# Attention with transposed scores: keys on the partitions, row maxima found in a pass of their own

## What is computed

```
xq = rms_norm(x @ wq.T, q_norm_w)         # 32 heads of 64
xk = rms_norm(x @ wk.T, k_norm_w)         # 8 key heads, each used by 4 query heads
xv = x @ wv.T
scores = einsum('bhtd,bhsd->bhts', xq, xk) / 8 + slope_h * (s - t)   # -inf unless 0 <= t - s <= 256
attn = softmax(scores)
out = einsum('bhts,bhsd->bhtd', attn, xv) @ wo.T
x = x + layernorm(out)
x = x + layernorm(ffn(layernorm(x)))      # silu(g) * u, inner width 1408
```

## Time and profile before

| what | value |
|---|---|
| median of 3 runs | 1387.37 us (1386.64 to 1392.79) |
| span of the profiled execution | 1386.5 us |
| PE busy | 1249.0 us (90%), 7996 products |
| DVE busy | 960.8 us (69%) |
| ACT busy | 797.8 us (58%) |
| POOL busy | 362.5 us (26%) |
| DMA | 180.36 MB, 130 GB/s over the span |

### The profile page before, as it was taken

The page is one execution under the profiler, slowest core; times in us unless marked ns, Lnnn a source line. Parts: engine busy times, 40 slices in busy tenths (PEclk is TensorE's granted clock), DMA queues, the critical chain, the costliest instruction groups (busy, mean ns, idle before and its releaser), DMA issues.

```text
span 1386.5 us, 28786 instructions
## 1 busy us (share of the span) xinstructions
PE 1249.0 (90%) x7996; PEld 1049.7 (76%) x7996; DVE 960.8 (69%) x2514; ACT 797.8 (58%) x2141; POOL 362.5 (26%) x443
## 2 busy tenths in 40 slices
PE   5999999985888899999999999999799998989894
PEld 4778787864677778888888888888677786868683
DVE  4587777668888887888888888888553665262623
ACT  3555454545788888888888888888322322222221
POOL 1000000010366664344344344344211001020201
PEclk9999999995799999999999999999899999999997
DMA  4226262556344453454443354343433322020100
GB/s 152 99 103 230 104 246 106 216 194 244 138 157 159 159 188 114 141 171 155 134 156 127 130 170 156 133 155 122 141 106 121 107 92 91 1 71 21 40 22 32
DMA packets 94444, 180.36 MB, mean 130 GB/s; under 512 B 7456, under 2 KB 36256, under 8 KB 94368
## 3 DMA queue, kind: packets, MB, share of 16 engines
q1 hardware_dynamic: 94368, 179.42, 37.2%
HBM read 107.83 MB, written 71.57 MB: 129 GB/s over the span
## 4 chain that ended last, share of the span: by engine, by line
PE 54%; issue 23%; DVE 10%; DMA 4%; ACT 4%; POOL 2%; SPq 1%; DVEq 1%; ACTq 0%; POOLq 0%
PE bank L1141 16%; PE bank L1206 13%; PE bank L1163 8%; PE bank L1172 7%; PE bank L1268 4%; PE bank L1184 3%; DMA v_st<-v_scr 3%; PE bank L1195 2%; DVE u_sb L951 2%; PE bank L1186 2%; DVE inv_rms L905 1%; DVE pT_lo L958 1%; ACT p_sb L747 1%; DMA o_in<-o_scr 1%; DVE o_raw L972 1%
## 5 line engine op out<-in xcount | busy, mean ns | idle before, releaser
L747 ACT ACTIVATE p_sb<-u_sb,low 128x384 f32<-128x384 f32 (+2 forms) x512 | 274.9, 537 | 70.5 <-DVE low L951 46.6
L951 DVE CUSTOM_DVE_ANT_0 u_sb<-bank,bias 128x384 f32<-128x384 f32 (+2 forms) x512 | 232.1, 453 | 69.0 <-PE bank L1163 49.5
L1163 PE MATMUL bank<-k_st,q_st 128*128 128x384 f32 (+2 forms) x1024 | 254.8, 331 | 17.0 <-DMA v_st<-v_scr 11.3
L1172 PE MATMUL bank<-ident,p_sb 128*128 128x128 f32 x1152 | 225.8, 288 | 45.1 <-DVE pT_lo L958 40.1
L958 DVE TENSOR_TENSOR pT_lo<-bank,pT_hi 128x384 f16<-128x384 f32 (+2 forms) x512 | 231.3, 452 | 21.4 <-ACT pT_hi L755 11.6
L755 ACT ACTIVATE pT_hi<-bank 128x384 f16<-128x384 f32 (+2 forms) x512 | 206.3, 403 | 47.4 <-PE bank L1172 42.9
L1163 PEld LDWEIGHTS bank<-k_st,q_st 128*128 128x128 f32 x1024 | 180.8, 197 | 42.7 <-issue 9.2
L1172 PEld LDWEIGHTS bank<-ident,p_sb 128*128 128x128 f32 x1152 | 141.9, 144 | 86.5 <-ACT p_sb L747 41.3
L1184 PE MATMUL bank<-v_st,pT_hi 128*128 128x128 f16 x1152 | 171.9, 224 | 0.7 <-DVE pT_lo L958 0.7
L1268 PE MATMUL bank<-zT_hi,gu 128*128 128x512 f32 x440 | 161.6, 400 | 3.0 <-issue 1.7
L554 POOL TENSOR_TENSOR o_mid<-o_raw,inv_sum 128x256 f32<-128x256 f32 x128 | 79.4, 620 | 314.7 <-DVE o_raw L972 314.7
(11 more groups left out here) (108 smaller groups left out, 2303.7 us busy)
## 6 DMA issues: line engine op xcount, KB each, us to landing
q_scr<-qk SPq DMA_DIRECT2D x64, 512.0 KB, 2.7
q_st<-q_scr SPq DMA_DIRECT2D x32, 1024.0 KB, 5.8
k_st<-k_scr SPq DMA_DIRECT2D x64, 256.0 KB, 3.0
o_scr<-o_out SPq DMA_DIRECT2D x128, 128.0 KB, 1.7
o_in<-o_scr SPq DMA_DIRECT2D x16, 1024.0 KB, 8.4
k_scr<-qk SPq DMA_DIRECT2D x16, 512.0 KB, 2.7
x_in<-x SPq DMA_DIRECT2D x4, 1024.0 KB, 8.1
w_stage<-wqT SPq DMA_DIRECT2D x4, 1024.0 KB, 6.5
```

The costliest lines, as they stand in the source:

```text
L747: nc.scalar.activation(p_sb[:, u % RING, 0:w], u_sb[:, u % RING, 0:w], ACT.Exp, scale=-1.0, bias=low[:, u % RING:u % RING + 1], accum_out= ...
L951: nc.vector.tensor_tensor_reduce(out=u_sb[:, u % RING, 0:w], in0=bank[u % 2][:, 0:w], in1=bias[:, 2 * u // UNITS, u % REP, at:at + w], sca ...
L1163: mm = nc.tensor.matmul(bank[u % 2][:, 0:w], q_st[:, s, r, P * i:P * i + P], k_st[:, s, part, P * key:P * key + w], start=(part == 0), sto ...
L1172: mm = nc.tensor.transpose(bank[2 + u % 2][:, P * j:P * j + P], p_sb[:, u % RING, P * j:P * j + P], ident[:])
```

## The change

The attention stage is built anew, and what feeds it with it.

- **Scores stand transposed**: keys on the partitions, 4 heads x 128 queries = 512 columns. A unit is one block of 128 keys x 128 queries for the four heads of a key head: 9 blocks per key head (`BLOCKS`), 18 units per n instead of 32. `scores` makes them with two products of 512 columns; the second one's 100 rows hold the low part of the keys and, as rows of the contraction, slopes, distances, the maxima and the window's mask (`k2`, `q2`).
- **Row maxima come from a pass of their own** (`max_entry`, `find_max`), one key head ahead: 16 products of 32 to 288 columns per key head, DVE's add-and-extreme on each, then two small transposes (`turn`), a copy on ACT and a round trip through DRAM to turn them into row 67 of `q2`. ACT issues these transfers (`copy_low`, `load_low`).
- **No transposes of the probabilities**. `exps` reads PSUM, POOL zeroes what lies outside the window (`mask`, six of nine blocks), ACT rounds to f16 (`round_p`), DVE (4 of 9 blocks) or POOL (5 of 9) takes the rest (`split_p`). `weigh_values` makes 12 products of 64 or 65 columns per block; the 65th column is a column of ones in the values and gives the row's sum, so that `finish_o` on DVE inverts and multiplies once.
- **The norm of the values** goes into `wo` (`split_wo`, now on ACT and DVE) instead of into every output.
- **Stores and loads**: `q_scr` holds rows of 2048 columns per key head. `store_qk` stores four query chunks at a time in four transfers; ACT's copy into `raw` waits until the same chunks of the previous batch are stored (`lo_stored`). Per key head 12 transfers load what were 4 (`load_km`, `load_k1`, `load_q1`, `load_q2`, `load_v`); the query rows of `q2` are loaded as 64 and 3. Constant rows are built in f32 by POOL and copied by DMA.
- At the end of attention, `load_o` for the first tile of the tail is issued after all output stores have landed.

```diff
-UNITS = 2 * TT * REP
+BLOCKS = [(i, j) for i in range(TT) for j in range(max(0, i - NB + 1), i + 1)]
+GUNITS = len(BLOCKS)
+UNITS = 2 * GUNITS
+DVE_SPLITS = (0, 1, 4, 7)
+LAGS = {"scores": 0, "exps": 0, "mask": 0, "round": 1, "split": 2, "weigh": 3, "finish": 4}
+MAX_STEPS = [[("max", 0), ("max", 1)], [("max", 2), ("max", 3)], ...
+RING = 6
...
@@ SP @@
+                elif f % REP == REP - 1:
+                    for half in range(2):
...
+                        sp.dma_start(q_scr[group, 0:HD].rearrange("a d n -> (a d) n"),
+                                     raw[rows, REP * j:REP * j + REP].rearrange("p c n -> p (c n)")).then_inc(lo_stored[j], DMA)
+                        sp.dma_start(q_scr[group, HD:2 * HD].rearrange("a d n -> (a d) n"), qk[rows, j % 2].bitcast(F32)).then_inc(hi_stored[j % 2], DMA)
...
+            def load_q2(n, s):
+                for a, b in ((0, HD), (HD, HD + 3)):
+                    sp.dma_start(q2[a:b, s].bitcast(F32),
+                                 q_scr[bass.ds(2 * n + s, 1), HD + a:HD + b].rearrange("g r t -> (g r) t")).then_inc(q2_loaded[s], DMA)
...
+            attend(B * TT - 1, (2, TT - 2), last=True)
+            store_o(B * TT - 1, 1, [2, 3])
             for i in range(TT):
                 sp.wait_ge(o_stored[i], DMA * 2 * B * TT)
+            load_o(B - 2, TT - 1)
@@ POOL @@
+            def mask(n, u):
...
+                pool.wait_ge(p_ready, UNITS * n + u + 1)
                 hold(pool)
+                nc.gpsimd.affine_select(out=p, in_=p, compare_op=ALU.is_ge, fill=0.0, base=0,
+                                        pattern=[[0, REP], [sign, P]], channel_multiplier=-sign).then_inc(masked, 1)
+
+            def split_p(n, u):
+                if u % GUNITS in DVE_SPLITS:
+                    return
+                pool.wait_ge(p_hi_ready, UNITS * n + u + 1)
+                nc.gpsimd.tensor_tensor(out=p_lo[:, u % RING], in0=p_sb[:, u % RING], in1=p_hi[:, u % RING], op=ALU.subtract).then_inc(p_split[0], 1)
@@ ACT @@
-                        at_least(act, qk_ready, (QC + KVC) * (b - 1) + n + 1)
-                        nc.scalar.activation(raw[:, n], bank[n % 4][:], ACT.Copy).then_inc(raw_ready, 1)
+                        at_least(act, lo_stored[n // REP], DMA * (2 if n < QC else 4) * b)
...
+                        nc.scalar.activation(raw_at(n), short(bank[n % 4][:]), ACT.Copy).then_inc(raw_ready, 1)
...
+            def copy_low(n, s, h, bank_at):
...
+                nc.scalar.activation(lowT[0:NQ // 2, h], bank[bank_at][0:NQ // 2, 0:P], ACT.Copy).then_inc(lowT_ready, 1)
+                act.wait_ge(lowT_ready, 2 * g + h + 1)
+                act.dma_start(q_scr[bass.ds(g, 1), ROWS - 1, 2 * T * h:2 * T * h + 2 * T].rearrange("g (q c) -> (g q) c", c=P),
+                              lowT[0:NQ // 2, h]).then_inc(low_stored[h], DMA)
+
+            def load_low(n, s, h):
+
+                act.wait_ge(low_stored[h], DMA * (2 * n + s + 1))
+                act.dma_start(q2[HD + 3:HD + 4, s, 2 * T * h:2 * T * h + 2 * T].bitcast(F32),
+                              q_scr[bass.ds(2 * n + s, 1), ROWS - 1, 2 * T * h:2 * T * h + 2 * T]).then_inc(low_loaded[s][h], DMA)
@@ DVE @@
+            def find_max(n, s, q, bank_at):
+
+                w = min(SHORT * (q + 1), MAXW)
...
+                dve.wait_ge(m_psum, NQ * (2 * n + s) + q + 1)
+                hold(dve)
+                nc.vector.tensor_tensor_reduce(out=u_sb[:, q % 2, 0:w], in0=bank[bank_at][:, 0:w], in1=bias[:, s, MAXW - w:MAXW], scale=1.0, scalar=BIG,
+                                               op0=ALU.add, op1=ALU.min, accum_out=low[:, s, q:q + 1]).then_inc(u_ready, 1)
@@ PE @@
+                at_least(pe, p_ready, UNITS * n + u - 1)
+                nc.tensor.matmul(bank[u % 2][:], k1[:, s, keys], q1[:, s, queries], start=True, stop=False)
+                nc.tensor.matmul(bank[u % 2][:], k2[0:FIXED, s, k2_at:k2_at + P], q2[0:FIXED, s, queries],
+                                 start=False, stop=True).then_inc(s_psum, 1)
...
+                for r in range(REP):
+                    hi, lo = (x[:, u % RING, P * r:P * r + P] for x in (p_hi, p_lo))
+                    nc.tensor.matmul(acc[:, r], hi, v_st[:, s, j, HD:2 * HD + 1], start=(first and r == 0), stop=False, skip_group_check=True)
+                    nc.tensor.matmul(acc[:, r, 0:HD], hi, v_st[:, s, j, 0:HD], start=False, stop=False, skip_group_check=True)
+                    mm = nc.tensor.matmul(acc[:, r], lo, v_st[:, s, j, HD:2 * HD + 1], start=False, stop=(i == j), skip_group_check=True)
                 mm.then_inc(pv_done, 1)
```

More of the change, by code:

```diff
@@ L116, in due, with tiles_due, splits_before, max_bank @@
         nn, uu = (n, u - lag) if u >= lag else (n - 1, UNITS + u - lag)
-        if uu < UNITS and not (isinstance(nn, int) and nn < 0) and (stage not in OF_FOUR_HEADS or uu % REP == REP - 1):
+        if uu < UNITS and not (isinstance(nn, int) and nn < 0) and (stage != "finish" or uu % GUNITS in TILE_ENDS):
             yield stage, nn, uu
+def tiles_due(tile, u):
+    if tile is None:
+        return
+    if u >= START:
+        yield tile, u - START
+    if u + UNITS - START < UNITS + 4 and not (isinstance(tile, int) and tile == 0):
+        yield tile - 1, u + UNITS - START
+def splits_before(n, u, on_dve):
+    one = len(DVE_SPLITS) if on_dve else GUNITS - len(DVE_SPLITS)
+    return one * (2 * n + u // GUNITS) + sum((k in DVE_SPLITS) == on_dve for k in range(u % GUNITS))
+def max_bank(entry, first):
+    return (4 if first else 2) + MAX_ORDER.index(entry) % 2
 def at_least(eng, sem, value):
@@ L769, in unit_work, with copy_y, tile_work @@
+            def copy_y(t):
+                act.wait_ge(oT_used, 4 * t + 4)
+                at_least(act, z_ready, t)
+                nc.scalar.activation(y_n[:], bank[7][:], ACT.Copy).then_inc(y_copied, 1)
             def unit_work(n, u):
                 for stage, nn, uu in due(n, u):
-                    work = {"transpose": round_pT, "exps": exps, "copy_low": copy_low}.get(stage)
+                    work = {"round": round_p, "exps": exps}.get(stage)
                     if work:
                         work(nn, uu)
-            def attend(n, tile=None):
+            def tile_work(tile, u):
+                for t, v in tiles_due(tile, u):
+                    m, at = divmod(v, 4)
+                    if m < 4 and at == 0:
+                        round_oT(t, m)
+                    if v == UNITS:
+                        copy_y(t)
@@ L776, in attend @@
+            def attend(n, tile=None, wo=False, last=False):
                 for u in range(UNITS):
                     unit_work(n, u)
+                    s, k = divmod(u, GUNITS)
+                    nn, ss = (n, 1) if s == 0 else (n + 1, 0)
+                    if not (last and s == 1):
+                        for kind, h in MAX_STEPS[k]:
+                            if kind == "turn":
+                                copy_low(nn, ss, h, max_bank((kind, h), False))
+                        if k == 6:
+                            load_low(nn, ss, 0)
+                    if k == 0:
+                        load_low(n, s, 1)
@@ new lines, in attend @@
+                    tile_work(tile, u)
+            dve.wait_ge(vn_loaded, 2 * DMA)
+            attend(0)
+            with dve.Fori(1, LAG) as n:
+                attend(n, wo=True)
+            attend(LAG, 0)
+            with dve.Fori(1, TT) as i:
+                attend(LAG + i, i)
+            with dve.Fori(0, TT) as i:
+                attend(LAG + TT + i, TT + i)
+            with dve.Fori(0, TT - 2) as i:
+                attend(LAG + 2 * TT + i, 2 * TT + i)
+            attend(B * TT - 1, 3 * TT - 2, last=True)
@@ new lines, in attend @@
+            def attend(n, tile=None, last=False):
+                for u in range(UNITS):
+                    unit_work(n, u, "scores")
+                    s, k = divmod(u, GUNITS)
+                    if not (last and s == 1):
+                        for entry in MAX_STEPS[k]:
+                            max_entry(*((n, 1) if s == 0 else (n + 1, 0)), entry)
+                    tile_work(tile, u)
+                    unit_work(n, u, "weigh")
+            pe.wait_ge(v_ready, TT * B)
+            pe.wait_ge(fixed_copied, 2 * (NB + 1) * DMA)
```

802 lines of the change are left out of this document (504 added, 298 removed).

## The result

The changed kernel took 1501.39 us (median of 4 runs, 1492.76 to 1517.22), the kernel before 1388.83 us (1386.64 to 1392.79): a ratio of 1.079, 95% interval 1.074 to 1.085. It is slower by 113 us, where 65 us less was forecast; the time lies far outside the range of 1272 to 1382 us.

What follows compares the result with a forecast made beforehand. PE was taken as the tightest engine in n = 5 to 15, ACT in n = 1 to 4, DVE in n = 0. Span: 1386.5 - 97 + 32 = 1321.5 us, so 1322 us forecast; range 1272 to 1382 us.

Steps and rivals of the forecast that it cites:

- (a): Projections: ACT's copy into `raw` waits for the previous batch's group of stores; 10 us more, ends 0 and 40.
- the rival that passes the waits through: Projections: the store waits of (a) pass through, 30 us more, 1352 us; chance 0.10.
- (b): Last batch's end: the first key head's maxima, 6.1 us of DVE, stand where DVE is late; 3 us more.
- (c): Attention's start: first key head's keys, `q2` and values are asked for only behind the last values' store; 8 us more.
- (d): Attention's end: the first tail tile's 1 MB load follows the landing of the last output stores; 9 us more.
- (e): The opening: scattered loads of the norm weights; 2 us more.
- Per n: Attention: 68 us less in n = 5 to 15, 20 in n = 1 to 4, 9 in n = 0; together 97.
- The rival that named it: Attention: ACT waits for the landing of the turned maxima four times per n; 122 us more, 1444 us; chance 0.08.
- Theory Q: From the experiments, not the prediction: SP's queue and the DMA engines are overloaded as a whole; no chance given.
- 5.9 us left: Kernel before, n = 5 to 15: PE's steps make 35.8 of 41.7 us; the rest are waits of 32 units.

Runs made afterwards that it cites:

- e4_nogate: Changed kernel with the second part of queries and keys stored from `qk`, so ACT's copy into `raw` need not wait; wrong values, measurement only: 1463.8 us.
- e7_inter2: Changed kernel with `q_scr` laid out anew, so a group's four 64-partition stores become two of 128 partitions by 8 KB: 1440.7 us.
- e10_spread: e9 with the first key head's maxima taken two per projection in the last five, eight entries behind the last, instead of four per projection: 1368.3 us.
- e9: e8 with the first key head's operands and the first tail tile's load asked for earlier, and its maxima row copied straight from `lowT`: 1373.2 us.
- e5: Changed kernel with the maxima row copied inside SBUF from `lowT` to `q2` from the second key head on, without the DRAM trip: 1454.7 us.
- e8: Changed kernel with the edits of e5 and e7 together, the row copied inside SBUF and two wide stores: 1393.8 us.
- e11: e8 with `q2`'s query load bringing one row instead of 64 from n = 1 on; wrong values, measurement only: 1394.3 us.
- e1: Changed kernel with a group's four stores made two of 128 partitions by 8 KB, DRAM side shaped 2 x 64 x 2048: 1927.3 us.

## Why the prediction was wrong

The terms of ACT, POOL and the value products stood; those of the transfers and of PE's long products behind short ones did not. Starts of the first product of each batch's projections and of the last one of all, from the timeline of PE:

| | batch 0 | 1 | 2 | 3 | last product | first exponential |
|---|---|---|---|---|---|---|
| before | 19.0 | 95.4 | 167.7 | 240.1 | 313.0 | 317.7 |
| changed | 19.2 | 96.0 | 185.9 | 277.2 | 389.1 | 406.7 |
| e4_nogate | 20.1 | 96.3 | 168.6 | 240.9 | 335.9 | 353.6 |
| e7_inter2 | 19.8 | 95.8 | 168.1 | 240.5 | 334.9 | 350.3 |
| e10_spread | 20.1 | 97.0 | 169.2 | 241.6 | 320.1 | 329.5 |

*(a), the waits for stores: 10 us taken, ends 0 and 40, measured 53.* Batch 1 takes 89.9 us instead of 72.3, batch 2 91.3 instead of 72.4, and of the 39 us more in the last batch 17 go with the gate (e4: 95.0 us against 111.9). **This is the first step that failed.** "One such store lands in 2.7 us" was no such store: the row's had 128 partitions, the new ones 64. They land in 6.0 and 7.4 us, SP's issue of one takes 1.9 us, and ACT's single waits reach 10.2 us, where the sum had 1.5 to 6. The mechanism and its place were right, and the rival that passes the waits through was too small by the same price. It takes both, the slow stores and the gate: with wide stores (e7) the gate stays and batches 1 and 2 take 72.3 and 72.4 us, the old pace, and without the gate (e4) they take 72.3 us with the narrow ones.

*(b), maxima in the last batch's end: 3 us taken, measured 22* (72.9 us in the kernel before, 95.0 without the gate). Only DVE's work was counted. It costs by order: PE's third product waits for a DVE that is behind a reciprocal. e10 wins 15 us with the same work; the last batch is still 6 us longer than before.

*(c), attention's start: 8 us taken, measured 13* (17.6 us from the last product, 4.7 before). The mechanism was right. The sum had 3 us for eight issues; SP needs 8.8 us from 392.25 on. The narrow stores explain only part of that: behind wide ones (e7) the same issues take 6.3 us, and attention starts 15.3 us after the last product. e9, which asks earlier, brings it to 3.0 us.

*(d), tail: 9 us taken, about 7 measured* (PE's idle time before it 8.0 us instead of the 0.93 of the earlier trace rows); *(e), opening: 2 taken, 0.6 measured* (batch 1 at 96.0 instead of 95.4). Right. The added terms come to 96 us instead of 32.

*Per n: 97 us less were forecast, and attention came out 32 us longer.* n = 0 took 53.4 us (49.5 forecast), n = 1 to 4 41.6 each (30.6), n = 5 to 15 42.7 (35.5): 127 us above the forecast. In e7, whose profiled execution is near its median, it is 105 us. These have two parts, and the rest, about 20 us, is for the most part that the changed kernel's profiled execution is its longest:

- **The round trip of the maxima is the second step that failed.** It costs 47 us of the total, in e5 against the changed kernel as in e8 against e7; in attention 60 us in the first pair, whose reference is that longest execution, and 42 in the second. The sum has no term for it. "The loads are asked for one key head (17 us) ahead, (...) so I cost them at nothing" holds for the operands from stage 1 and not for this row: its second half is turned in the last unit of the key head before, and its load is asked for in the first unit of the key head that needs it. The rival that named it had a chance of 0.08 and was half right. ACT's wait, which it priced, is 31 us in all, and 66 in e7, far from its 122; what it left out is that the load that follows needs another 5 us at 608.88, and that a key head's scores from the fourth unit on stand behind it (PE waits 51 us for it, and 41 in e7). How much of the 47 us goes with either wait was not separated. Theory Q is out: with the trip gone, fewer bytes win nothing (e11).
- *The other 63 us, which e8 still has, are PE's own steps and the units' chain.* In e8 PE's steps add up to 39.8 us per n at n = 6 to 13, against 31.5 forecast plus 4 of waits: scores 12.3 us instead of 8.3 (0.32 for the first product instead of 0.23, and waits for DVE behind the second), maxima 5.7 instead of 3.9, values 7.1 instead of 6.1, transposes and output 14.4 instead of 12.8. Here the step from the earlier trace rows was taken for a product that has short ones before it. The same misreading stands in the sum for the kernel before: of the "5.9 us left" as waits PE is idle for only 2.4 us per n at n = 6 to 13; the rest are longer steps. For n = 1 to 4 (37.2 instead of 30.6 us) ACT's busy share was carried over from before, though ACT is busy for only about 60% there in e8; PE's clock is 0.77 of full in the changed kernel and 0.82 in e8, and each unit passes through five engines. How much each of these two has was not separated and stays open.

The parts close: 96 us of added terms and 32 us of attention are 128 of the 129 us between the two spans. Two of the rivals, the store waits and the round trip, came true together, where the chances had them as alternatives.

## What to carry to other kernels

Take the price of a transfer from a row with the same number of partitions, not with the same number of bytes, and look at the slowest dimension of both sides before it is written. A value that goes out to DRAM and back within a loop is two landings long and goes on the chain as such; if both ends lie in SBUF, one transfer does. Where an engine waits in order for one of two banks, count entries per visit of the engine that frees them, and not busy time.

## What the runs showed of the hardware that was not expected

- A transfer of partitions 0 to 63 or 64 to 127 has little over half the rate: packets of 8 KB took 0.592 us on average with 64 partitions and 0.322 with 128, that is 13.8 and 25.4 GB/s in each DMA engine. The Trainium skill (SBUF — State Buffer, Door 1: The DMA port swizzle) says that partitions 0 to 63 reach 8 of the 16 ports; the runs agree. Lower and upper half were stored in turn here, and the rate stayed at that of one half.
- A leading dimension of 2 made the same bytes take so long that attention began 387 us later (e1 against e7).
- SP's issue is part of the price. That of `qk`'s stores took 0.40 us behind wide stores, 1.94 us in the median behind narrow ones, 2.39 at most.
- ACT's issue of the 4 KB row into one partition of SBUF took 0.64 us, of the store to DRAM 0.30, and the shorter way still won 47 us.
- Value products of 64 and 65 columns with new 16-bit weights step 0.03 us in a row at full clock and 0.055 at half.
